# Language-model tower in one kernel: identifiers in two transfers of 128 equal rows, the shift made in the one-hot

## Chip, cores and metric

One core of one Trainium2 chip. The metric is the device time of one execution in microseconds (us); lower is better.

## What is computed

16 sequences of 128 identifiers (0 to 63) and 128 positions go through a token encoder, a diagonal state-space layer and a feed-forward layer with 8 experts, all in float32. The start of the encoder is what matters here:

```python
amps = emb[byte_sequence]
onehot = jnp.transpose(jax.nn.one_hot(byte_sequence, 64), (0, 2, 1))
h = gelu(conv1d(onehot, w1, b1, 3))         # 64 -> 128, 7 taps
h = gelu(conv1d(h, w2, b2, 2))              # 128 -> 64, 5 taps
ctx = sigmoid(conv1d(h, w3, b3, 1))[:, 0, :]
amps = amps * ctx[:, :, None]
lp = locality_shapes[byte_sequence]
center = byte_pos[None, :] + lp[..., 0] * 0.05
xd = continuous_positions[:, None, :] - center[..., None]
...                                         # 4 scales:
z = xd / width[..., None]
basis = exp(-0.5 * z * z) * cos(phase + TWO_PI * z)
...
field = einsum('bsp,bsd->bpd', basis_total, amps)
```

Then `h = field`, `h = h + attn(layernorm(h))`, `h = h + ffn(layernorm(h))`.

## The kernel before, in words

Each engine has its own list of instructions, written out by hand, and runs it strictly in order; semaphores join the lists. The 16 sequences are worked in G = 4 groups of GB = 4 (512 columns), so stage names carry a group: `z(g)`, `product(g)`, `field(g)`.

**Loads.** SyncE issues all loads in a row (L261 to L270): the identifiers twice, w1, positions of group 0 ("pos0"), positions of the others ("pos"), w2, the state constants, wd, bd. ScalarE's queue loads the small constants (L414). The identifiers go to partitions 0 to 63 and again to 64 to 127, each time all 2048 of them, repeated into 64 rows of 8 KB; the lower half of the tile `ids` holds them one element later than the upper half.

**One-hot.** VectorE compares identifiers with the partition's value. `onehot_b` (bf16, 64 partitions, L641) feeds the look-ups: TensorE multiplies it by three bf16 parts of the table, first for the 4 locality shapes (L935 to L937, 48 matmuls), then for the embeddings (`embeddings(q)`, 24 matmuls each). `onehot` (128 partitions, padded, L645 to L649) feeds `conv1`: its upper half is the same one-hot shifted by one position, so that one matmul serves two taps. Its pads are cleared by GpSimd (L299, L300).

**TensorE** fills gaps with `keep_warm(n, bank)`: n matmuls of 512 columns whose result nobody reads (L921). Its list begins: keep_warm(14), look-ups of shapes, keep_warm(3), embeddings(0), keep_warm(3), conv1 of groups 0 and 1, conv1 of groups 2 and 3 (8 matmuls a group, in two parts of w1), conv2(0) (L965), embeddings(1), tap(0), keep_warm(10), context(0), keep_warm(8), conv2(1), keep_warm(4), field(0), keep_warm(6), upright(0), field(1), tap(1), and so on. `upright(g)` transposes the field back (L1004) after ScalarE's `field_out(g)` (L500) copied it; ScalarE's `upright_out(g)` (L504) then writes `h_a`.

**ScalarE** copies the shapes (L442), takes the tanh of one of them (L444), rounds w1 to its first part (L446), negates the centre (L448), then forms the distances of groups 1 to 3 (`distances(g)`, L455, four activations each, all waiting for "pos"). Between these stand conv1_out (L460, gelu), square (L466). Then conv2_out(0) (L482), the exp table, gaussian (L470), cosine (L476, sine table), square(2), cosine(2), field_out(0), load_gelu, upright_out(0), conv2_out(1), load_exp, field_out(1), taps_out(1), gaussian(2), upright_out(1), context_out(1) (L495). `load_gelu`, `load_exp` and `load_sin` run a one-column activation (L425) whose function makes the engine load its table (1.28 us) at that place.

**VectorE**, after the one-hot, forms w1's second part (L651), centre (L655), widths, phase and their reciprocals, the distances of group 0 (L669), and then z(0), z(1), turns(0), turns(1), z(2), turns(2), gates(0), product(0), product(1), z(3), moments(0, 0), turns(3), normalise(0, 0), gates(1), product(2) and on. `z` is L675; `turns` is four operations of phase and wrap (L685) and one mask (L690); `gates(q)` (L715, L722) needs context_out(q); `product` is L732; `moments(0, 0)` (L744, L747) needs `h_a` of group 0; GpSimd then computes the reciprocal standard deviation (L379 to L386) and `normalise(0, 0)` (L754) uses it.

Of the kernel before, what the change touches and what calls it, by code (L numbers as in the profile page):

```python
# [15 lines left out]
ALU = mybir.AluOpType  # L16
ACT = mybir.ActivationFunctionType
F32 = mybir.dt.float32
# [4 lines left out]
P = 128  # L23
# [48 lines left out]
def tower(nc, x, positions, small, w1, w2, state, wd, bd, out):  # L72
    ctx = ExitStack()
    with ctx:
# [27 lines left out]
        ids = sb("ids", [P, NB * P + 2], I32)  # L102
# [29 lines left out]
        center = sb("center", [P, NB])  # L132
# [82 lines left out]
        s_onehot = sem("s_onehot")  # L215
        s_w1_part = sem("s_w1_part")
        s_center, s_warm = sem("s_center"), sem("s_warm")
# [40 lines left out]
        @block.sync  # L258
        def _(sp):
            row = x.rearrange("b t -> (b t)")  # L260
            for half in range(2):  # L261
                sp.dma_start(ids[half * V:half * V + V, 1 - half:1 - half + NB * P],
                             repeat(row, 0, V)).then_inc(ld[f"x{half}"], 16)
            sp.dma_start(w1_sb[:, :, :], w1).then_inc(ld["w1"], 16)
            sp.dma_start(posb[:, 0:GB, :], repeat(positions[0:GB], 0, P)).then_inc(ld["pos0"], 16)
            sp.dma_start(posb[:, GB:, :], repeat(positions[GB:], 0, P)).then_inc(ld["pos"], 16)
            sp.dma_start(w2_sb[:, :, :], w2).then_inc(ld["w2"], 16)
            sp.dma_start(st_sb[:, :], state).then_inc(ld["state"], 16)
            sp.dma_start(wd_sb[:, :, :], wd).then_inc(ld["wd"], 16)
            sp.dma_start(bd_sb[:, :], bd[0].rearrange("(p c) -> p c", p=P)).then_inc(ld["bd"], 16)  # L270
            sp.wait_ge(s_bd_split, 1)
            for half in range(2):
                for k in range(3):
                    row = half * D + k
                    sp.dma_start(bdp[row:row + 1, :].rearrange("o (p c) -> o p c", p=P),
                                 bd_parts[:, k, :]).then_inc(ld["bias"], 16)
            for g in range(G - 1):
                sp.wait_ge(s_result, g + 1)
                sp.dma_start(out[g * GB:(g + 1) * GB].rearrange("b p d -> p b d"),
                             result[:, g]).then_inc(stored, 16)  # L280
            for h in range(2):
                sp.wait_ge(s_last, 2 * h + 2)
                sp.dma_start(out[(G - 1) * GB + h:G * GB:2].rearrange("b p d -> p b d"),
                             result[:, G - 1, h:GB:2]).then_inc(stored, 16)
            sp.wait_ge(stored, 16 * (G + 1))
# [127 lines left out]
        def _(act):  # L413
# [4 lines left out]
            act.activation(half_b3[:, :], col("b3"), ACT.Copy, scale=0.5).then_inc(s_halfb3, 1)  # L418

# [20 lines left out]
            load_gelu()  # L440
            act.wait_ge(s_shapes_mm, 1)
            act.copy(shapes[:, :, :].rearrange("p b c -> p (b c)"), bank[6][:, 0:NB * NL]).then_inc(s_shapes, 1)  # L442
            act.wait_ge(s_shapes, 1)
            act.activation(amp_tanh[:, :], shapes[:, :, 2], ACT.Tanh, scale=0.5).then_inc(s_amp_tanh, 1)  # L444
            act.wait_ge(ld["w1"], 16)
            act.copy(w1p[0][:], w1_sb[:]).then_inc(s_w1_part, 1)  # L446
            act.wait_ge(s_center, 1)
            act.activation(neg_center[:, :], center[:, :], ACT.Copy, scale=-1.0).then_inc(s_negc, 1)  # L448
            act.wait_ge(s_negc, 1)

            def distances(g):

                act.wait_ge(ld["pos"], 16)
                for b in range(g * GB, (g + 1) * GB):
                    ins = act.activation(dist[:, b, :], posb[:, b, :], ACT.Identity, bias=neg_center[:, b:b + 1])  # L455
                ins.then_inc(s_rest[g], 1)
# [83 lines left out]

            distances(1)
            conv1_out(0)
            distances(2)
# [22 lines left out]
            field_out(0)  # L566
            load_gelu()
            upright_out(0)
# [50 lines left out]
        def _(dve):  # L619
            count = [0]  # L620

            def link(ins):
# [15 lines left out]
            dve.wait_ge(ld["x0"], 16)  # L638
            from_first, from_zero = (ids[:, k:k + NB * P].rearrange("p (b t) -> p b t", b=NB) for k in (1, 0))
            value = col("value")  # L640
            dve.tensor_scalar(onehot_b[:, :, :], from_first[0:V], value[0:V], None,  # L641
                              ALU.is_equal).then_inc(s_onehot, 1)
            dve.wait_ge(ld["x1"], 16)
            dve.wait_ge(s_pad, 2)
            dve.tensor_scalar(onehot[:, :, 3:2 + P], from_first[:, :, 0:P - 1], value, None, ALU.is_equal)  # L645
            dve.tensor_scalar(onehot[0:V, :, 2 + P:3 + P], from_first[0:V, :, P - 1:P], value[0:V], None,
                              ALU.is_equal)
            dve.tensor_scalar(onehot[V:, :, 2:3], from_zero[V:, :, 0:1], value[V:], None,
                              ALU.is_equal).then_inc(s_onehot, 1)  # L649
            dve.wait_ge(s_w1_part, 1)  # L650
            dve.tensor_tensor(w1p[1][:], w1_sb[:], w1p[0][:].bitcast(F32), ALU.subtract).then_inc(s_w1_part, 1)  # L651

            dve.wait_ge(s_shapes, 1)
            lp = [shapes[:, :, k] for k in range(NL)]
            dve.tensor_scalar(center[:, :], lp[0], 0.05, col("place"), ALU.mult, ALU.add).then_inc(s_center, 1)  # L655
            link(dve.scalar_tensor_tensor(out=absw[:, :], in0=lp[1], scalar=-1.0, in1=lp[1], op0=ALU.mult, op1=ALU.max))
            for s in range(NS):
                c = SMALL["widths"].start + s
                ins = dve.tensor_scalar(width[:, :, s, :], absw[:, :].rearrange("p (g b) -> p g b", g=G),
                                        sm[:, c:c + 1], 1e-5, ALU.mult, ALU.add)  # L660
            link(ins)
# [3 lines left out]
            dve.scalar_tensor_tensor(out=phase[:, :], in0=lp[3], scalar=0.5, in1=phase_tmp[:, 1, :],  # L665
                                     op0=ALU.mult, op1=ALU.subtract)
            dve.wait_ge(ld["pos0"], 16)
            dve.wait_ge(s_center, 1)
            link(dve.tensor_tensor(dist[:, 0:GB, :], posb[:, 0:GB, :], repeat(center[:, 0:GB], 2, P), ALU.subtract))  # L669

            def z(g):

                if g:
                    dve.wait_ge(s_rest[g], 1)
                dve.tensor_tensor(  # L675
                    wave[:, g, :].rearrange("p (s t) -> p s t", s=NS),
                    repeat(dist[:, g * GB:(g + 1) * GB, :].rearrange("p b t -> p (b t)"), 1, NS),
                    repeat(inv_width[:, g, :, :].rearrange("p s b -> p (s b)"), 2, P),
                    ALU.mult).then_inc(s_z[g], 1)

            def turns(g):
# [7 lines left out]
                link(ins)  # L689
                dve.tensor_scalar(angle[:, g, :], angle[:, g, :], TURN_MASK, None,  # L690
# [163 lines left out]
            turns(0)  # L854
            turns(1)
            z(2)
            turns(2)
# [3 lines left out]
            z(3)  # L861
            moments(0, 0)
            turns(3)
# [53 lines left out]
        def _(pe):  # L917
# [6 lines left out]
            keep_warm(14, 7)  # L924

            pe.wait_ge(s_emb_split, 1)
            pe.wait_ge(s_onehot, 1)
# [7 lines left out]
            for b in range(NB):  # L935
                mm = look_up(bank[6][:, b * NL:(b + 1) * NL], b, slice(D, D + NL))
# [192 lines left out]
            pe.wait_ge(s_onehot, 2)  # L1129
            conv1((0, 1))  # L1130
            conv1((2, 3))
# [143 lines left out]
```

## Time and profile before

| | us |
|---|---|
| runs, median (lowest to highest) | 111.62 (111.35 to 115.62) |
| the profiled execution | 111.52 |
| its span in the profile | 109.6 |
| busy TensorE, VectorE, ScalarE, GpSimd | 100.5, 90.0, 70.8, 51.0 |

All durations below are of the one profiled execution. The span is the time from the first to the last recorded instruction; the rest of the execution's time lies around it. TensorE's busy time holds the keep_warm matmuls.

### The profile page before, as it was taken

How to read it: one execution, taken by the hardware profiler on the slowest of the kernel's cores; microseconds unless marked ns; L12 is line 12 of the kernel's file. 1: busy time of each engine (PE TensorE's matmuls, PEld its weight loads, DVE VectorE, ACT ScalarE, POOL GpSimd, SP SyncE). 2: the span in 40 equal slices, each digit the busy share in tenths (PEclk: the TensorE clock that was granted, in tenths of full speed). 3: DMA queues.
4: the chain of work that ended last, by engine and by line, in shares of the span. 5: the costliest groups of instructions: out<-in, count | busy, mean ns of one | idle time of the engine just before them, and what ended most of it. 6: DMA issues, size and time to landing. Idle time of an engine off the chain costs nothing.

```text
span 109.6 us, 2018 instructions
## 1 busy us (share of the span) xinstructions
PE 100.5 (92%) x723; PEld 64.3 (59%) x723; DVE 90.0 (82%) x230; ACT 70.8 (65%) x126; POOL 51.0 (47%) x101
## 2 busy tenths in 40 slices
PE   5979999999999978869899999999999799999970
PEld 2356785364434576347567477876696476776640
DVE  0359999999999949999999599678999956199892
ACT  4604599999999999999869438454758513551000
POOL 7798998899980007205509426256005000000670
PEclk9999999999999999999999999999999999999999
DMA  3999700000000100000000000000000000000044
GB/s 91 269 233 408 283 0 0 3 0 0 6 0 4 5 0 0 0 0 6 0 0 0 0 6 0 0 0 0 0 0 9 0 0 0 0 0 0 0 96 96
DMA packets 4313, 4.15 MB, mean 38 GB/s; under 512 B 3280, under 2 KB 3536, under 8 KB 4176
## 3 DMA queue, kind: packets, MB, share of 16 engines
q1 hardware_dynamic: 4160, 3.92, 12.5%
q10 hardware_dynamic: 144, 0.12, 0.4%
q8 instruction: 5, 0.08, 0.3%
q14 instruction: 4, 0.03, 0.1%
HBM read 3.50 MB, written 0.52 MB: 37 GB/s over the span
## 4 chain that ended last, share of the span: by engine, by line
PE 42%; ACT 38%; DVE 8%; DMA 4%; issue 4%; POOL 2%; ACTq 0%; DVEq 0%
PE pair L1080 14%; ACT wave L476 8%; PE bank L1042 7%; ACT bell L466 7%; ACT bell L470 5%; ACT L425 5%; DMA ids<-x 4%; DVE pair L819 3%; PE hid_pair L1053 3%; PE pair L951 3%; ACT angle L514 3%; PE pair L921 2%; ACT h L460 2%; PE hid_pair L1063 2%; ACT dist L455 2%
## 5 line engine op out<-in xcount | busy, mean ns | idle before, releaser
L379 POOL TENSOR_SCALAR var_eps<-mean_var 128x4 f32<-128x4 f32 x8 | 3.7, 458 | 33.0 <-DVE mean_var L747 33.0
L819 DVE COPY_PREDICATED pair<-later,pair 128x256 f32<-128x256 int32 (+3 forms) x30 | 12.3, 409 | 5.3 <-PE pair L1080 4.6
L921 PE MATMUL pair<-warm 128*128 128x512 bf16 x53 | 13.3, 380 | 0.0
L732 DVE SCALAR_TENSOR_TENSOR bell<-bell,scale_w,wave 128x512 f32<-128x512 f32 x16 | 10.8, 743 | 0.0
L1080 PE MATMUL pair<-wd_high,H_high 128*128 128x512 f32 x32 | 10.8, 418 | 0.0
L921 PE MATMUL hid_pair<-warm 128*128 128x512 bf16 x30 | 9.0, 455 | 1.3 <-POOL warm L298 1.3
L1080 PE MATMUL pair<-wd_low,H_high 128*128 128x512 f32 x32 | 10.0, 394 | 0.0
L395 POOL TENSOR_TENSOR angle<-picked,prob 128x256 f32<-128x256 f32 x3 | 1.8, 613 | 17.2 <-DVE prob L843 17.2
L521 ACT ACTIVATE bell<-hid_pair,sm 128x512 f32<-128x512 f32 x8 | 5.0, 680 | 7.2 <-PE hid_pair L1053 7.2
L675 DVE TENSOR_TENSOR wave<-dist,inv_width 128x2048 f32<-128x2048 f32 x4 | 9.3, 2356 | 0.0
L965 PE MATMUL pair<-h,w_sb 128*64 128x512 f32 x40 | 9.1, 597 | 0.0
L1080 PE MATMUL pair<-wd_high,H_low 128*128 128x512 f32 x32 | 9.0, 402 | 0.0
L476 ACT ACTIVATE wave<-angle,neg_pi 128x1024 f32<-128x1024 int32 x8 | 8.6, 1138 | 0.1
L385 POOL TENSOR_TENSOR rstd<-var_eps,minus_half 128x4 f32<-128x4 f32 x6 | 8.2, 1366 | 0.0
L685 DVE TENSOR_SCALAR angle<-wave,phase 128x512 int32<-128x512 f32 x16 | 8.0, 561 | 0.0
L921 PEld LDWEIGHTS pair<-warm 128*128 128x128 bf16 x53 | 4.9, 102 | 5.2 <-issue 1.3
L951 PE MATMUL pair<-onehot,w1p 128*128 128x512 f32 x32 | 7.9, 404 | 0.0
L996 PE MATMUL pair<-bell,amps 128*64 128x128 f32 x128 | 7.9, 276 | 0.0
L425 ACT ACT_TABLE_LOAD x6 | 7.7, 1283 | 0.1
L996 PEld LDWEIGHTS pair<-bell,amps 128*64 128x64 f32 x128 | 6.9, 137 | 1.3 <-issue 1.3
L470 ACT ACTIVATE bell<-bell 128x2048 f32<-128x2048 f32 x4 | 7.6, 1920 | 0.0
L466 ACT ACTIVATE bell<-wave 128x2048 f32<-128x2048 f32 x4 | 7.6, 1910 | 0.0
(166 smaller groups left out, 226.1 us busy)
## 6 DMA issues: line engine op xcount, KB each, us to landing
ids<-x SPq DMA_DIRECT2D x2, 512.0 KB, 5.7
posb<-positions SPq DMA_DIRECT2D x1, 768.0 KB, 8.1
wd_sb<-wd SPq DMA_DIRECT2D x1, 512.0 KB, 9.1
out<-angle SPq DMA_DIRECT2D x3, 128.0 KB, 2.0
st_sb<-state SPq DMA_DIRECT2D x1, 328.0 KB, 8.3
w_sb<-w SPq DMA_DIRECT2D x1, 256.0 KB, 6.6
posb<-positions SPq DMA_DIRECT2D x1, 256.0 KB, 6.6
w_sb<-w SPq DMA_DIRECT2D x1, 160.0 KB, 8.0
```

Source lines behind the costliest of these rows:

```text
L425: act.activation(unused[:, k:k + 1], neg_pi[:, :], function)
L466: act.activation(bell[:, g, :], wave[:, g, :], ACT.Square).then_inc(s_square[g], 1)
L470: act.activation(bell[:, g, :], bell[:, g, :], ACT.Exp, scale=-0.5).then_inc(s_bell[g], 1)
L476: act.activation(wave[:, g, part], angle[:, g, part], ACT.Sin, bias=neg_pi[:, 0:1], scale=2.0 * PI_BELOW / TURN).then_inc(s_cos[g], 1)
L675: dve.tensor_tensor(wave[:, g, :].rearrange("p (s t) -> p s t", s=NS), repeat(dist[:, g * GB:(g + 1) * GB, :].rearrange("p b t -> p (b t)" ...
L732: ins = dve.scalar_tensor_tensor(out=bell[:, g, part], in0=bell[:, g, part], scalar=scale_w[:, s:s + 1], in1=wave[:, g, part], op0=ALU.mul ...
L819: return dve.copy_predicated(held[:, :, 0:n, 0, 0:D], repeat(later[:, g, 2 * h + rows.start:2 * h + rows.stop, first:first + n], 3, D), he ...
L921: pe.matmul(bank[free], warm[:, 0:P], warm[:, :], start=True, stop=True)
L951: mm = pe.matmul(bank[g], w1p[part][:, j, :], onehot[:, g * GB:(g + 1) * GB, 2 * j:2 * j + P], start=(part == 0 and j == 0), stop=(part == ...
L965: mm = pe.matmul(bank[2 * q][r * D:(r + 1) * D, :], w2_sb[:, k, :], h1[:, g * GB:(g + 1) * GB, k:k + P], start=(k == 0), stop=(k == K2 - 1))
L996: mm = pe.matmul(bank[g][r * D:(r + 1) * D, c * P:(c + 1) * P], amps[:, g * GB + b, :], bell[:, g, at:at + P], start=(s == 0), stop=(s == ...
L1080: mm = pe.matmul(pair[h][:, jj, :], hidden_part[:, g % 2, k, cols], weights[:, k, :], start=False, stop=last and k == KH - 1)
```

## The change

- Identifiers: two transfers again, but each carries half of the text (8 sequences, 1024 identifiers) to all 128 partitions, in rows of 4 KB; `ids` is no longer shifted.
- One-hot by halves of the text: VectorE makes `onehot_b` (64 partitions) and then the upper, shifted rows of `onehot` (the shift is now in where it writes). ScalarE copies `onehot_b` to the lower rows. conv1 waits for both, by halves.
- TensorE: 11 warm-up matmuls at the start in place of 14; the shape look-ups in two halves with 4 warm-up matmuls between; embeddings(0) stays before conv 1.
- VectorE makes the negated centre itself (with a negated place that ScalarE prepares early), and w1's second part after the widths. ScalarE makes all four groups' distances, group 0 waiting only for "pos0"; the order is distances(0), amp tanh, distances(1), distances(2), conv1_out(0).
- `turns` is split into `phases` and `wrap`, which follow each other but for group 3: z(3), phases(3), moments(0, 0), wrap(3).
- ScalarE: upright_out(0) stands before load_gelu in place of behind it.

```diff
@@ sync
-            for half in range(2):
-                sp.dma_start(ids[half * V:half * V + V, 1 - half:1 - half + NB * P],
-                             repeat(row, 0, V)).then_inc(ld[f"x{half}"], 16)
+            for part in range(2):
+                n = slice(part * NB * P // 2, (part + 1) * NB * P // 2)
+                sp.dma_start(ids[:, n], repeat(row[n], 0, P)).then_inc(ld[f"x{part}"], 16)
@@ scalar
+            act.activation(neg_place[:, :], col("place"), ACT.Copy, scale=-1.0).then_inc(s_place, 1)
...
+            act.wait_ge(s_pad, 2)
+            for part in range(2):
+                n = slice(part * NB // 2, (part + 1) * NB // 2)
+                act.wait_ge(s_onehot, part + 1)
+                act.copy(onehot[0:V, n, 3:3 + P], onehot_b[:, n, :]).then_inc(s_lower, 1)
             act.wait_ge(s_shapes_mm, 1)
             act.copy(shapes[:, :, :].rearrange("p b c -> p (b c)"), bank[6][:, 0:NB * NL]).then_inc(s_shapes, 1)
             act.wait_ge(s_shapes, 1)
-            act.activation(amp_tanh[:, :], shapes[:, :, 2], ACT.Tanh, scale=0.5).then_inc(s_amp_tanh, 1)
             act.wait_ge(ld["w1"], 16)
             act.copy(w1p[0][:], w1_sb[:]).then_inc(s_w1_part, 1)
-            act.wait_ge(s_center, 1)
-            act.activation(neg_center[:, :], center[:, :], ACT.Copy, scale=-1.0).then_inc(s_negc, 1)
             act.wait_ge(s_negc, 1)
...
-                act.wait_ge(ld["pos"], 16)
+                act.wait_ge(ld["pos" if g else "pos0"], 16)
...
+            distances(0)
+            act.activation(amp_tanh[:, :], shapes[:, :, 2], ACT.Tanh, scale=0.5).then_inc(s_amp_tanh, 1)
             distances(1)
+            distances(2)
             conv1_out(0)
-            distances(2)
             conv1_out(1)
...
             field_out(0)
+            upright_out(0)
             load_gelu()
-            upright_out(0)
             conv2_out(1)
@@ vector
-            dve.wait_ge(ld["x0"], 16)
-            from_first, from_zero = (ids[:, k:k + NB * P].rearrange("p (b t) -> p b t", b=NB) for k in (1, 0))
+            ids_rows = ids[:, :].rearrange("p (b t) -> p b t", b=NB)
             value = col("value")
-            dve.tensor_scalar(onehot_b[:, :, :], from_first[0:V], value[0:V], None,
-                              ALU.is_equal).then_inc(s_onehot, 1)
-            dve.wait_ge(ld["x1"], 16)
-            dve.wait_ge(s_pad, 2)
-            dve.tensor_scalar(onehot[:, :, 3:2 + P], from_first[:, :, 0:P - 1], value, None, ALU.is_equal)
-            dve.tensor_scalar(onehot[0:V, :, 2 + P:3 + P], from_first[0:V, :, P - 1:P], value[0:V], None,
-                              ALU.is_equal)
-            dve.tensor_scalar(onehot[V:, :, 2:3], from_zero[V:, :, 0:1], value[V:], None,
-                              ALU.is_equal).then_inc(s_onehot, 1)
-            dve.wait_ge(s_w1_part, 1)
-            dve.tensor_tensor(w1p[1][:], w1_sb[:], w1p[0][:].bitcast(F32), ALU.subtract).then_inc(s_w1_part, 1)
+            for part in range(2):
+                n = slice(part * NB // 2, (part + 1) * NB // 2)
+                dve.wait_ge(ld[f"x{part}"], 16)
+                dve.tensor_scalar(onehot_b[:, n, :], ids_rows[0:V, n], value[0:V], None,
+                                  ALU.is_equal).then_inc(s_onehot, 1)
+                if part == 0:
+                    dve.wait_ge(s_pad, 2)
+                dve.tensor_scalar(onehot[V:, n, 2:2 + P], ids_rows[V:, n], value[V:], None,
+                                  ALU.is_equal).then_inc(s_upper, 1)
...
+            dve.wait_ge(s_place, 1)
-            dve.tensor_scalar(center[:, :], lp[0], 0.05, col("place"), ALU.mult, ALU.add).then_inc(s_center, 1)
+            dve.tensor_scalar(neg_center[:, :], lp[0], -0.05, neg_place[:, 0:1], ALU.mult,
+                              ALU.add).then_inc(s_negc, 1)
...
+            dve.wait_ge(s_w1_part, 1)
+            dve.tensor_tensor(w1p[1][:], w1_sb[:], w1p[0][:].bitcast(F32), ALU.subtract).then_inc(s_w1_part, 1)
...
-            link(dve.tensor_tensor(dist[:, 0:GB, :], posb[:, 0:GB, :], repeat(center[:, 0:GB], 2, P), ALU.subtract))
...
             z(3)
+            phases(3)
             moments(0, 0)
-            turns(3)
+            wrap(3)
             normalise(0, 0)
@@ tensor
-            keep_warm(14, 7)
+            keep_warm(11, 7)
             pe.wait_ge(s_emb_split, 1)
-            pe.wait_ge(s_onehot, 1)
...
-            for b in range(NB):
-                mm = look_up(bank[6][:, b * NL:(b + 1) * NL], b, slice(D, D + NL))
+            for part in range(2):
+                pe.wait_ge(s_onehot, part + 1)
+                for b in range(part * NB // 2, (part + 1) * NB // 2):
+                    mm = look_up(bank[6][:, b * NL:(b + 1) * NL], b, slice(D, D + NL))
+                if part == 0:
+                    keep_warm(4, 7)
             mm.then_inc(s_shapes_mm, 1)
...
-            pe.wait_ge(s_onehot, 2)
+            pe.wait_ge(s_lower, 1)
+            pe.wait_ge(s_upper, 1)
             conv1((0, 1))
+            pe.wait_ge(s_lower, 2)
+            pe.wait_ge(s_upper, 2)
             conv1((2, 3))
```

## Rows read from the trace of the kernel before

**Rows 1.** Chain of waits that ended last: start us, us, what; its first transfer.
```profile
0.72 4.86 DMA ids<-x
```

**Rows 2.** DMA issues: out<-in engine op xcount, KB each, us from issue to landing.
```profile
posb<-positions SPq DMA_DIRECT2D x1, 768.0 KB, 8.1
...
posb<-positions SPq DMA_DIRECT2D x1, 256.0 KB, 6.6
```

**Rows 3.** Timeline of SyncE's queue and TensorE: start us, us, engine, line, op.
```profile
1.30 5.07 PE L921 MATMUL hid_pair<-warm 128*128 128x512 bf16 x14 [1.30 <-POOL warm L298]
...
2.62 0.43 SPq L265 DMA_DIRECT2D posb<-positions  x1
3.09 0.44 SPq L266 DMA_DIRECT2D posb<-positions  x1
...
5.11 0.76 PEld L921 LDWEIGHTS hid_pair<-warm 128*128 128x128 bf16 x4 [0.28 <-issue]
...
8.34 0.82 PE L921 MATMUL hid_pair<-warm 128*128 128x512 bf16 x3
...
10.36 7.90 PE L951 MATMUL pair<-onehot,w1p 128*128 128x512 f32 x32
...
18.19 4.52 PE L965 MATMUL pair<-h,w_sb 128*64 128x512 f32 x20
```

**Rows 4.** Timeline of VectorE up to z(0) and z(1).
```profile
5.61 1.31 DVE L641 TENSOR_SCALAR onehot_b<-ids,sm 64x2048 bf16<-64x2048 int32 x1 [1.54 <-DMA ids<-x]
7.95 1.30 DVE L645 TENSOR_SCALAR onehot<-ids,sm 128x2032 fp32r<-128x2032 int32 x1 [1.03 <-DMA ids<-x]
...
10.29 0.23 DVE L655 TENSOR_SCALAR center<-shapes,sm 128x16 f32<-128x16 f32 x1
...
13.07 4.52 DVE L675 TENSOR_TENSOR wave<-dist,inv_width 128x2048 f32<-128x2048 f32 x2
```

**Rows 5.** Timeline of ScalarE: conv1_out(0), distances(2), conv2_out(0), a cast of 128x1024.
```profile
13.59 0.69 ACT L460 ACTIVATE h<-pair,sm 128x512 f32<-128x512 f32 x1 [1.05 <-PE pair L951]
14.18 1.27 ACT L455 ACTIVATE dist<-posb,neg_center 128x128 f32<-128x128 f32 x4
...
22.91 0.69 ACT L482 ACTIVATE h<-pair,sm 128x512 f32<-128x512 f32 x1
...
57.95 1.03 ACT L589 CAST wd_high<-wd_sb 128x1024 fp32r<-128x1024 f32 x1
```

**Rows 6.** Busy time by stretch: stretch, PE busy (x) PEld DVE ACT POOL, PEclk, DMA, GB/s.
```profile
22.90:38.60 15.70, 15.15 (x116) 7.53 (x111) 15.56 (x19) 15.55 (x17) 9.33 (x13) 1.00 0.04 3
...
46.30:53.60 7.30, 5.90 (x49) 3.49 (x48) 7.20 (x20) 6.84 (x9) 2.97 (x4) 1.00 0.01 2
```

**Rows 7.** Timeline of ScalarE and VectorE, 38 to 46 us.
```profile
38.52 0.35 ACT L500 COPY angle<-pair 128x256 f32<-128x256 f32 x1
...
40.29 0.35 ACT L504 COPY h_a<-pair 128x256 f32<-128x256 f32 x1
40.54 0.69 ACT L482 ACTIVATE h<-pair,sm 128x512 f32<-128x512 f32 x1
40.68 0.60 DVE L744 BATCH_NORM_STATS2 stats<-h_a 128x6 f32<-128x64 f32 x4 [1.45 <-ACT h_a L504]
...
41.61 1.64 DVE L685 TENSOR_SCALAR angle<-wave,phase 128x512 int32<-128x512 f32 x4
...
44.59 0.98 DVE L754 TENSOR_SCALAR angle<-h_a,mean_var,rstd 128x64 f32<-128x64 f32 x4
...
45.05 0.29 ACT L495 ACTIVATE ctx_tanh<-hid_pair,half_b 128x8 f32<-128x8 f32 x1
...
45.49 0.16 DVE L715 SCALAR_TENSOR_TENSOR gain<-ctx_tanh,amp_tmp 128x8 f32<-128x8 f32 x1
```

**Rows 8.** Timeline of ScalarE: field_out(3) and upright_out(3) without a table load between them.
```profile
60.58 0.35 ACT L500 COPY angle<-pair 128x256 f32<-128x256 f32 x1
...
61.47 0.38 ACT L504 COPY h_a<-pair 128x256 f32<-128x256 f32 x1
```

More of the change, by code:

```diff
@@ L101, in tower @@
         posb = sb("posb", [P, NB, P])
-        ids = sb("ids", [P, NB * P + 2], I32)
+        ids = sb("ids", [P, NB * P], I32)
         def col(name):
@@ L131, in tower @@
         amps = sb("amps", [P, NB, D])
-        center = sb("center", [P, NB])
+        neg_place = sb("neg_place", [P, 1])
         absw = sb("absw", [P, NB])
@@ L214, in tower @@
         s_emb_split = sem("s_emb_split")
-        s_onehot = sem("s_onehot")
+        s_onehot, s_lower, s_upper = sem("s_onehot"), sem("s_lower"), sem("s_upper")
         s_w1_part = sem("s_w1_part")
-        s_center, s_warm = sem("s_center"), sem("s_warm")
+        s_place, s_warm = sem("s_place"), sem("s_warm")
         s_copied = [sem("s_copied0"), sem("s_copied1")]
@@ L664, in _ @@
             link(dve.tensor_scalar(phase_tmp[:, 1, :], phase_tmp[:, 0, :], -ROUND, -0.75, ALU.add, ALU.add))
[L665 to L668, printed above, removed]
-            link(dve.tensor_tensor(dist[:, 0:GB, :], posb[:, 0:GB, :], repeat(center[:, 0:GB], 2, P), ALU.subtract))
+            link(dve.scalar_tensor_tensor(out=phase[:, :], in0=lp[3], scalar=0.5, in1=phase_tmp[:, 1, :],
+                                          op0=ALU.mult, op1=ALU.subtract))
             def z(g):
-                if g:
-                    dve.wait_ge(s_rest[g], 1)
+                dve.wait_ge(s_rest[g], 1)
                 dve.tensor_tensor(
@@ L679, in z, with phases @@
                     ALU.mult).then_inc(s_z[g], 1)
-            def turns(g):
+            def phases(g):
                 dve.wait_ge(s_z[g], 1)
@@ L689, in turns, with wrap @@
                 link(ins)
+            def wrap(g):
                 dve.tensor_scalar(angle[:, g, :], angle[:, g, :], TURN_MASK, None,
@@ L853, in _ @@
             z(1)
-            turns(0)
-            turns(1)
-            z(2)
-            turns(2)
+            phases(0)
+            wrap(0)
+            phases(1)
+            wrap(1)
+            z(2)
+            phases(2)
+            wrap(2)
             gates(0)
```

## Prediction

> **What bounds the kernel now.** I read the chain of waits first. It begins with the identifiers' transfer, issued at 0.72 and landed at 5.58 [rows 1]. The busy times by stretch show what leads then: ScalarE is busy for 15.55 of the 15.70 us from 22.9 to 38.6, VectorE for 7.20 of the 7.30 from 46.3 to 53.6 [rows 6], and behind it the chain stays mostly on TensorE. So the question is in two parts: how much earlier can ScalarE get into its long run (conv2_out(0), at 22.91 [rows 5]), and does what it gains there live until VectorE's product(2) at 46.3, behind which everything later hangs?
>
> For the second part I read the timeline around 38 to 46 us. There two engines are level. ScalarE ends context_out(1) at 45.34; VectorE takes it up in gates(1) at 45.49, when its own normalise(0, 0) (44.59, 0.98 long) is just over [rows 7]. A change must move both to move the end.
>
> **The transfers.** The two transfers of now carry 512 KB each (64 partitions, rows of 8 KB). The first lands at 5.58; the second at 7.93, since VectorE's wait for it ends at 7.95 [rows 4]: 2.35 us, 223 GB/s. The two loads of positions, repeated rows as well but on 128 partitions, land at 2.62 + 6.6 = 9.2 and 3.09 + 8.1 = 11.2: 768 KB in 2.0 us, 393 GB/s [rows 2, 3]. At that pace 512 KB take 1.33 us. The new first transfer should land about 1 us of moving earlier; as part of its 4.86 us is start-up, shared with the small constants, I take 0.7 of it: 4.9. The second comes 1.33 later, 6.2. Bounds: no faster than now (5.58 and 7.93), or all of the first's gain (4.6 and 5.9).
> The Trainium skill's SBUF page (SBUF — State Buffer, Door 1: the DMA port swizzle) says that 64 partitions reach half of the ports, for about 218 GB/s, and 128 all, for 436; by it 512 KB would take 1.2 us. Its DMA page (DMA: Bandwidth & Descriptors, Specifications) speaks against so much: about 358 GB/s from HBM, which would make it 1.46 us. The trace's 393 lies between, and is measured.
>
> **One-hot on VectorE.** Now 64x2048 takes 1.31 us and 128x2032 1.30 [rows 4]. Four operations of 64x1024 replace them: half of 1.31 is 0.66, all of it would be 1.31; I take 0.76, a little over half for the fixed part. The first half's bf16 one-hot is ready at 4.93 + 0.76 = 5.69, its upper rows at 6.4, the second bf16 half at 7.1 (the second transfer has long landed), its upper rows at 7.8. Now the last piece ends at about 9.65.
>
> **TensorE up to conv 1.** Warm-up matmuls come first, 11 in place of 14. The 14 took 5.07 us from 1.30; weight loads come every 0.43 us up to 5.11, where the last four begin together [rows 3]. So ten run at 0.427 (1.2 GHz for 512 columns) and four in 0.8 (2.4 GHz); I go by these steps. Eleven end at 1.30 + 4.27 + 0.2 = 5.78: however early the identifiers come, nothing starts sooner. By the one-hot, the first 24 look-ups start at 5.69 + 0.14 = 5.83. The 48 take 1.28 us (7.06 to the next warm-up at 8.34), so 24 take 0.64: 6.47. Then four warm-ups at 0.25: 7.47. Then 24 more: 8.11. From there to conv 1 all is as now, 3 warm-ups, 24 look-ups, 3 warm-ups, 8.34 to 10.36 = 2.02 [rows 3]. Conv 1 starts at 10.13, which is 0.23 us earlier; at best, by the 5.78, 0.28.
> Conv 1's other inputs come in time. ScalarE's lower-row copies, 64x1024, have 128x1024 as nearest row, 1.03 us [rows 5]: 5.7 to 6.75 and 7.1 to 8.15. The look-ups' copy follows at 8.2 and takes 0.2, then the first part of w1, half the length of that row, some 0.6: done by 9.1. VectorE's second part of w1, moved behind the widths, ends by 10.4 and is asked for 2 us into conv 1. If the copies took twice as long, w1 would be ready at about 10.2 to 11.2 and conv 1 up to 1 us late; that end I keep for the range.
>
> **VectorE and ScalarE up to conv2_out(0).** VectorE goes from centre to z(0) in 13.07 - 10.29 = 2.78 [rows 4]. It starts at about 8.5, loses the distances (128x512) and gains the w1 part (128x512, two inputs as well): z(0) at 11.3, 1.8 us earlier. distances(0), new on ScalarE, needs four activations, 1.27 us as distances(2) does [rows 5], from 9.15 to 10.4, and delays nothing. ScalarE waited 1.05 us for conv 1 at 13.59 [rows 5]; this gap takes distances(2) and the rest. With conv 1 at 10.13 it does conv1_out(0) at 13.3, square(0) at 14.9, conv1_out(2, 3) by 19.15, and would reach conv2_out(0) at 22.05, some 0.9 us earlier. But the convolution itself isn't there: conv 2 starts straight behind conv 1, at 18.19, and ends at 22.71 [rows 3], so now at 22.48. conv2_out(0) starts at 22.51 and not at 22.91: **gain 0.40 us**, and 0.5 us of ScalarE's lead goes into a wait on TensorE.
>
> **ScalarE 22.9 to 45.3.** All stays in order and without idle [rows 6] up to field_out(0), which comes 0.40 earlier (38.12). Here the change pulls upright_out(0) in front of the load of the gelu table. Now ScalarE hides TensorE's transposes behind that 1.28 us load: field_out(0) at 38.52, upright_out(0) at 40.29, conv2_out(1) at 40.54, a step of 2.02 [rows 7]. Where upright_out follows field_out with no load between, the second starts 0.89 after the first (60.58 and 61.47) [rows 8]. From a copy over a table load to the next operation it is 1.77 (38.52 to 40.29). The new step is 0.89 + 1.77 = 2.66: **loss 0.64 us**. The cover is gone and nothing takes its place. Sum at conv2_out(1): -0.40 + 0.64 = +0.24. Its tap and context follow in the same order, so context_out(1) ends at 45.58.
>
> **VectorE 39 to 46.** It waited 1.45 us, from 39.23, for h_a(0) [rows 7]. Now phases(3) (1.64) stands in that wait, and h_a(0) is ready at about 39.3. Even with z(3) not earlier, moments(0, 0) begins at 40.87; GpSimd's rstd then takes the 2.9 us of now or, with VectorE quiet, less. normalise(0, 0) ends between 44.7 and 45.7, so the context decides: gates(1) at 45.6 in place of 45.49, **+0.1 us**. VectorE's lead of up to 1.8 us turns into waits there. The new wait of ScalarE for the transposes has conv2_out(1), tap(1) and context(1) queued behind it; this is its price, already counted.
> From product(2) on the order and the work are the same, VectorE and then TensorE bound, and all shifts by that 0.1. phases and wrap are the same instructions under two names; field, experts and the tail are untouched. Field_out(1) to cosine(3) on ScalarE are 0.24 late, with cosine(3) done by about 53.1 while product(3) reads its first half at 53.4: free.
>
> **Sum.** The profiled execution took 111.52, with 109.6 of span and 1.9 around it; it stands 0.1 under the median of 111.62. 111.52 + 0.1 gives **111.6 us**, no change that can be told. Its own range, from the 4.6 landing and the 0.64 in full or two thirds of it, is 111.2 to 112.0.
>
> **Rivals.**
> A. *The identifiers don't come faster, and the split costs*: what sets their pace would be the repeated read or the count of rows, not the partitions. For it: twice the rows to handle; against: the 393 GB/s of positions. Landings 5.58 and 7.93; second bf16 half at 7.95 + 0.76 = 8.7; look-ups end at 9.5; conv 1 at 11.5, +1.1. conv2_out(0) is then at 23.6 to 23.8 (+0.9 at most, since conv 2 had 0.2 of lead), plus 0.64 for the table load, makes context_out(1) +1.5: **113.0**, slower. It decides as soon as the second one-hot half is later than 7.3, when TensorE begins to wait. VectorE in a full-length 1.31 us for 64x1024 comes to the same place.
> B. *The wait for the upright copy isn't paid*: were the transposes ready when ScalarE asks, the 0.40 would go through. ScalarE at 44.94, VectorE ready at 44.7 to 44.9, gates(1) at 44.95, 0.54 earlier: **111.0**. For it: VectorE waited 1.45 us for this very result, so it was wanted sooner. Against: TensorE can't begin before field_out(0), and the 0.89 step [rows 8] is bare latency.
> C. *The whole lead of VectorE counts* (1.8 us, 109.7), if the chain's pieces on ScalarE were only parallel. Against: ScalarE has no idle from 22.9 to 38.9, and gates(1) must have the context.
>
> **Chances.** Forecast 0.62, A 0.15, B 0.18, C 0.05. The range goes from 110.8 (below B) to 113.0 (A's time, and most of the late copies). A difference of 2% is about what a measurement of this kernel can tell from none; faster by more (under 109.4) has 0.04, between C and nothing; slower by more (over 113.85) 0.04, if A and late copies add up; within 0.92.
>
> **What would show it.** Right: the first one-hot operation near 4.9 and the second half's near 6.4; conv 1's first matmul at 10.1; z(0) at 11.3; ScalarE idle for about 0.5 us in front of conv2_out(0), at 22.5, and again in front of upright_out(0) on its way to the table load; conv2_out(1) near 40.8; VectorE idle ahead of gates(1) near 45.6. Wrong: conv 1 after 10.5 (A); conv2_out(1) before 40.3 (B); product(2) before 45.5.

## The result: slower by 3.6%, and the profile after

| | before | changed |
|---|---|---|
| median of the runs, us | 111.53 | 116.47 |
| lowest to highest | 111.35 to 115.62 | 114.73 to 118.08 |
| the profiled execution | 111.52 | 116.83 |
| its span | 109.6 | 114.7 |

Four executions of each kernel stand in the table (three of the kernel before in the table ahead of the prediction, hence 111.62 there). The ratio is 1.0355, 95% interval 1.0205 to 1.0505; forecast was 111.6. The ratio leaves out the two most disturbed of the changed kernel's four runs, the profiled one among them; its spread and TensorE's mean granted clock, 0.956 to 0.985 in the four, are part of what is explained below.

First the DMA issues of the changed kernel (KB each, us from issue to landing):

```profile
ids<-x SPq DMA_DIRECT2D x2, 512.0 KB, 5.1
...
sm<-small ACTq DMA_DIRECT2D x1, 116.0 KB, 4.8
```

The identifiers did what was forecast: 4.6 and 5.5 us from issues at 0.72 and 1.15, so 5.3 and 6.6, 1.3 us apart (forecast 4.9 and 6.2, 1.33 apart). But the small constants, 116 KB on ScalarE's queue, landed at 5.54. In the kernel before, the same load landed at 2.83. The DMA queues' packets, MB and busy share from 1.5 to 2.5 us show how, first before, then changed (q1 is SyncE's queue, q10 ScalarE's; the share is of the time of 16 DMA engines):

```profile
q1 hardware_dynamic: 16, 0.13, 59.7%
q10 hardware_dynamic: 144, 0.12, 46.6%
```

```profile
q1 hardware_dynamic: 42, 0.17, 50.0%
q10 hardware_dynamic: 11, 0.01, 8.2%
```

Before, all 144 packets of the constants pass in this microsecond; changed, 11 of them, and the last one only after 5.0. Two chains start from them: VectorE's split of the table, without which there are no look-ups, and GpSimd's some 25 operations on one column each (L325 to L351) that compute the coefficients of the state-space layer, here called the poles. ScalarE's `decay` activation, which stands ahead of conv2_out(0), waits for the poles. Timeline of the changed kernel, VectorE and TensorE:

```profile
5.56 0.19 DVE L636 CAST embp<-sm 64x68 bf16<-64x68 f32 x1 [5.56 <-DMA sm<-small]
...
6.72 0.74 DVE L648 TENSOR_SCALAR onehot_b<-ids,sm 64x1024 bf16<-64x1024 int32 x1
...
7.61 0.74 PE L939 MATMUL hid_pair<-embp,onehot_b 64*128 64x4 bf16 x24 [1.43 <-DVE onehot_b L648]
...
9.95 1.46 PE L930 MATMUL hid_pair<-warm 128*128 128x512 bf16 x3
...
11.34 1.46 PE L939 MATMUL bank<-embp,onehot_b 64*128 64x64 bf16 x24
...
13.63 9.17 PE L963 MATMUL pair<-onehot,w1p 128*128 128x512 f32 x32
22.73 4.52 PE L977 MATMUL pair<-h,w_sb 128*64 128x512 f32 x20
```

TensorE, done with its 11 warm-ups, idled 1.43 us ahead of the first look-ups (1.8 us later than forecast). From 9.95 on it ran at half pace: three warm-ups in 1.46 us against 0.82 [rows 3]. The busy times by stretch of the changed kernel (PEclk is the first number behind POOL's) name it:

```profile
8.00:10.00 2.00, 2.00 (x43) 1.30 (x41) 1.75 (x3) 1.54 (x2) 1.89 (x3) 0.91 1.01 369
10.00:12.00 2.00, 2.00 (x17) 0.89 (x17) 1.67 (x9) 1.97 (x7) 1.82 (x4) 0.50 0.88 344
12.00:14.00 2.00, 2.00 (x19) 1.27 (x17) 1.90 (x5) 2.00 (x9) 1.71 (x4) 0.50 0.07 21
14.00:16.00 2.00, 2.00 (x6) 1.63 (x5) 2.00 (x2) 0.55 (x2) 1.92 (x2) 0.50 0.00 0
16.00:18.00 2.00, 2.00 (x9) 1.56 (x9) 2.00 (x3) 0.00 (x0) 2.00 (x2) 0.88 0.00 0
```

The granted clock is at its lower level, 1.2 GHz, for some 7 us. Conv 1 starts at 13.63 in place of 10.36 and takes 9.17 in place of 7.90. The next fence has one operation of GpSimd's chain in the kernel before; the one behind it has that operation and the next of the changed kernel, and its ScalarE:

```profile
9.93 0.88 POOL L339 TENSOR_TENSOR spar<-spar,minus_half 128x1 f32<-128x1 f32 x1
```

```profile
12.96 2.69 POOL L339 TENSOR_TENSOR spar<-spar,minus_half 128x1 f32<-128x1 f32 x1
15.73 1.74 POOL L340 TENSOR_TENSOR spar<-spar 128x1 f32<-128x1 f32 x1
...
26.37 0.73 ACT L557 ACTIVATE decay<-decay,spar 128x512 f32<-128x512 f32 x1 [0.68 <-POOLq L352]
...
27.48 0.67 ACT L485 ACTIVATE h<-pair,sm 128x512 f32<-128x512 f32 x1
...
43.06 0.35 ACT L503 COPY angle<-pair 128x256 f32<-128x256 f32 x1
43.94 0.37 ACT L507 COPY h_a<-pair 128x256 f32<-128x256 f32 x1 [0.53 <-PE pair L1016]
...
45.73 0.67 ACT L485 ACTIVATE h<-pair,sm 128x512 f32<-128x512 f32 x1
```

VectorE of the changed kernel, gates(1):

```profile
50.53 0.17 DVE L720 SCALAR_TENSOR_TENSOR gain<-ctx_tanh,amp_tmp 128x8 f32<-128x8 f32 x1 [0.74 <-ACT ctx_tanh L498]
```

conv2_out(0) is 4.57 us late against 22.91 [rows 5]. From there the forecast's sum holds to a tenth: 4.57 and 0.64 for the transposes, less the 0.15 that VectorE had to spare, is 5.06. gates(1) is 5.04 late (50.53 against 45.49 [rows 7]), the span 5.1.

### The profile page after: what moved, and what is told of

The parts are those of the page before. It is cut to its first block, busy times and chain, and to the rows that moved or that the text cites. A ratio compares the mean times of both kernels' runs of the same rounds, so it can differ in the third digit from the quotient of the medians.

```text
span 114.7 us, 2029 instructions
## 1 busy us (share of the span) xinstructions
PE 104.0 (91%) x724; PEld 66.2 (58%) x724; DVE 87.3 (76%) x229; ACT 74.1 (65%) x132; POOL 50.8 (44%) x101
## 4 chain that ended last, share of the span: by engine, by line
PE 35%; ACT 23%; POOL 19%; DVE 11%; issue 5%; DMA 4%; ACTq 0%; POOLq 0%; DVEq 0%
PE pair L1092 14%; PE bank L1054 6%; ACT wave L479 6%; DMA sm<-small 4%; ACT L426 3%; DVE pair L824 3%; POOL spar L347 3%; ACT bell L473 3%; PE hid_pair L1065 3%; ACT angle L517 2%; DVE bell L737 2%; POOL spar L339 2%; PE pair L930 2%; PE hid_pair L1075 2%; PE bank L1037 2%
## 5 line engine op out<-in xcount | busy, mean ns | idle before, releaser
L930 PE MATMUL hid_pair<-warm 128*128 128x512 bf16 x31 | 11.1, 516 | 1.3 <-POOL warm L298 1.3
L737 DVE SCALAR_TENSOR_TENSOR bell<-bell,scale_w,wave 128x512 f32<-128x512 f32 x16 | 10.9, 745 | 1.4 <-ACT wave L479 1.4
L963 PE MATMUL pair<-onehot,w1p 128*128 128x512 f32 x32 | 9.2, 450 | 0.0
L963 PEld LDWEIGHTS pair<-onehot,w1p 128*128 128x128 f32 x32 | 7.0, 220 | 2.0 <-issue 0.3
```

The lines of the kernel that those rows point to most:

```text
L737: ins = dve.scalar_tensor_tensor(out=bell[:, g, part], in0=bell[:, g, part], scalar=scale_w[:, s:s + 1], in1=wave[:, g, part], op0=ALU.mul ...
L930: pe.matmul(bank[free], warm[:, 0:P], warm[:, :], start=True, stop=True)
L963: mm = pe.matmul(bank[g], w1p[part][:, j, :], onehot[:, g * GB:(g + 1) * GB, 2 * j:2 * j + P], start=(part == 0 and j == 0), stop=(part == ...
```

## Experiments

Each ratio is to the kernel before, run beside the experiment: its median was 111.45 beside e1 to e4, 111.58 beside e5, e6, e7 and e10, and 112.51 beside e8 and e9, each group on a chip of its own. Times of single stages are of the one profiled execution.

**Constants first, on the same queue.** e1, the changed kernel with:

```diff
@@ sync
+            sp.dma_start(sm[:, :], small).then_inc(ld["small"], 16)
@@ scalar
-            act.dma_start(sm[:, :], small).then_inc(ld["small"], 16)
```

> The changed kernel, with the small constants loaded as the first transfer of SyncE's queue and no longer from ScalarE's. Theory 1 (the constants, 116 KB, are mixed with the identifiers' rows and land at 5.54 instead of 2.83; all that starts from them is late): they land by about 3.2, the first look-ups start at 5.8 to 6.2, TensorE is never at half clock, conv 1 starts at 10.1 to 10.5, and the time is 111.3 to 112.2, as was forecast for the change. Theory 2 (the split one-hot with its ScalarE copies and 11 warm-ups costs by itself): conv 1 still at half clock or after 12, the time 114 or more.

```profile
2.89 0.19 DVE L636 CAST embp<-sm 64x68 bf16<-64x68 f32 x1 [2.89 <-DMA sm<-small]
...
6.29 0.74 PE L939 MATMUL hid_pair<-embp,onehot_b 64*128 64x4 bf16 x24 [0.48 <-DVE onehot_b L648]
...
10.64 7.88 PE L963 MATMUL pair<-onehot,w1p 128*128 128x512 f32 x32
```

Profiled 112.81, span 110.2, ratio 1.0079 (1.0013 to 1.0146). The constants land early, conv 1 runs at full clock. Conv 1's start is 0.14 outside the expected interval, since the identifiers, now behind the constants, land at 5.4; the time is 0.6 above its interval. Theory 1 holds for the bulk: 4.0 of the 5.3 us between the profiles are gone. But of six runs two took 115.4 and 115.6 with a mean clock of 0.97, which was not expected: early constants alone don't make the kernel safe.

**More warm-ups.** e2, the changed kernel with `keep_warm(18, 7)` for `keep_warm(11, 7)` at the start.

> The changed kernel with 18 warm-up matmuls in place of 11 at the start, so that TensorE's idle 1.4 us before the first look-ups is gone while the constants are as late as before. If the fall of the clock comes from that idle time: no stretch at half clock, conv 1 starts near 11.8 in place of 13.6 and takes 7.9 us in place of 9.2. If it comes from the low activity of the warm-ups and look-ups as such, the clock falls all the same. For the time: if TensorE's late conv 1 was the only thing that held conv2_out(0), the time falls by about 3 us, to 112 to 113; if GpSimd's chain of poles (ready at 26.3, also started by the late constants) holds ScalarE's decay just as late, conv2_out(0) stays near 27.3 and the time within 0.5 us of the changed kernel's.

```profile
5.57 0.19 DVE L636 CAST embp<-sm 64x68 bf16<-64x68 f32 x1 [5.57 <-DMA sm<-small]
...
11.97 7.87 PE L963 MATMUL pair<-onehot,w1p 128*128 128x512 f32 x32
...
26.36 0.72 ACT L557 ACTIVATE decay<-decay,spar 128x512 f32<-128x512 f32 x1 [3.65 <-POOLq L352]
27.46 0.67 ACT L485 ACTIVATE h<-pair,sm 128x512 f32<-128x512 f32 x1
```

TensorE's idle time before the look-ups shrank to 0.38 us and conv 1 ran at full clock, 1.7 us earlier and 1.3 shorter. In the profiled execution it brought nothing: ScalarE waited 3.65 us for GpSimd's poles, and conv2_out(0) stayed at 27.46. Profiled 117.18. From 22 to 30 us, where TensorE now idled 3.1 us, the mean granted clock was 0.94, and from 46 to 53 us 0.76. Three of the four runs took 117.2 to 118.7. The fourth, not profiled, took 113.86 with a clock of 1.00; its span of 111.8 leaves no room for conv2_out(0) as late as that, and why isn't known.

**Both holds away.** e10, the same 18 warm-ups, and ScalarE's three activations on GpSimd's values (`decay` and two `C_part`, L552 to L555 of the kernel before) moved from ahead of conv2_out(0) to behind cosine(1).

> The changed kernel with 18 warm-up matmuls, and with ScalarE's decay and C_part activations, which wait for GpSimd's poles, moved from ahead of conv2_out(0) to behind cosine(1). Constants are late as in the changed kernel. If the clock and the poles were the two holds on conv2_out(0), it starts near 24.4 (conv 2's end) in place of 27.48, and the time falls by about 2.5 to 3.3 us against the changed kernel, to 113.3 to 114.3. If only one of the two or a third one held it, it stays at or above 26.

```profile
24.16 0.69 ACT L485 ACTIVATE h<-pair,sm 128x512 f32<-128x512 f32 x1 [1.62 <-PE pair L977]
...
40.86 0.35 ACT L503 COPY angle<-pair 128x256 f32<-128x256 f32 x1
```

Profiled 114.65, 2.2 less than changed, runs 114.54 to 115.64, ratio to before 1.0303 (1.0269 to 1.0337): the start of conv2_out(0) is 0.24 earlier than expected, the time 0.35 above its interval, the gain 0.3 short. The rows have the missing part: conv2_out(0) came 3.3 us earlier, but the three moved activations now stand behind it, and field_out(0) starts 16.7 us after it in place of 15.6. So there were two holds, the half clock and the poles. That the poles alone are late enough is e2. That the half clock alone is, no run of the changed kernel's load order shows, but two others do: in e5 and e6 below the constants and the poles were early, TensorE went at half pace, and conv2_out(0) waited for conv 2 until 27.90. In the changed kernel itself conv 2 ends at 27.25.

**Warm-ups alone.** e3, the kernel before with `keep_warm(11, 7)` for `keep_warm(14, 7)`.

> The kernel before with 11 warm-up matmuls in place of 14: TensorE then idles about 1.0 to 1.3 us (5.8 or 6.2 to 7.06) with the constants early and everything else as it was. If an idle stretch at this point takes the clock down, conv 1 runs partly at half clock, starts up to 1.5 us later and ends up to 4 us later, time 113 to 115.5. If the clock stays: 111.5, no change.

```profile
8.00:10.00 2.00, 2.00 (x25) 0.92 (x22) 1.95 (x4) 0.95 (x3) 1.86 (x3) 0.60 1.08 430
10.00:12.00 2.00, 2.00 (x24) 1.36 (x21) 1.90 (x10) 1.02 (x4) 1.73 (x6) 0.55 1.02 389
```

Profiled 112.82, median 113.05, ratio 1.0145 (1.0115 to 1.0176); the interval began at 113. TensorE idled 1.36 us to 7.00, the granted clock was at its lower level from about 8.4 to 11.8, conv 1 started at 11.84, as expected. Three dummy matmuls less cost 1.3 us between the profiles and 1.45% by the ratio, in a kernel that is otherwise the same.

**Rows of 64 partitions.** e4, the changed kernel with the transfers of before:

```diff
-                sp.dma_start(ids[:, n], repeat(row[n], 0, P)).then_inc(ld[f"x{part}"], 16)
+                sp.dma_start(ids[part * V:part * V + V, :],
+                             repeat(row, 0, V)).then_inc(ld[f"x{part}"], 16)
```

(VectorE's waits follow: both halves of `onehot_b` wait for the first transfer, the upper rows for the second.)

> The changed kernel with the two transfers of the kernel before (whole text, 64 partitions, 8 KB rows); one-hot, copies and order stay as changed, the upper rows wait for the second transfer. Theory 1: the constants land again near 2.8, TensorE idles little and the clock stays, conv 1 near 11.3 to 12 for lack of the second half's one-hot, the time 112.5 to 113.5. If the constants are late for another reason (their own queue, the earlier issue of the later loads), they land at 5 or later here too and the time is 115 or more.

```profile
2.87 0.19 DVE L636 CAST embp<-sm 64x68 bf16<-64x68 f32 x1 [2.87 <-DMA sm<-small]
...
9.51 0.75 PE L940 MATMUL hid_pair<-embp,onehot_b 64*128 64x4 bf16 x24 [1.38 <-DVE onehot_b L648]
...
13.76 7.90 PE L964 MATMUL pair<-onehot,w1p 128*128 128x512 f32 x32
```

The constants land early again, from the same queue at the same instant, so it is the new form of the identifiers' transfers beside them that held them up. Which part of the form, 128 partitions for 64 or rows of 4 KB for 8, isn't separated: e4 takes back both. (The loads behind go back to their old issue times too, w1 to 2.00 from 1.63, but the 42 packets of SyncE's queue that pass first in the changed kernel carry 4 KB each, as the identifiers' rows do.) The expectations for TensorE and the time missed (profiled 115.43, ratio 1.0381, 1.0314 to 1.0448): the upper rows had to wait for the second transfer at 7.9, VectorE's second half stood behind them, TensorE idled 1.38 us until 9.5, and the granted clock fell behind that (0.58 and 0.56 from 10 to 14 us); conv 1 started at 13.76 and not by 12. I had left the clock out of that sum.

**Who is issued first.** e6, the changed kernel; SyncE waits for GpSimd's first memset ahead of the identifiers:

```diff
+            sp.wait_ge(s_warm, 1)
```

> The changed kernel; SyncE waits for GpSimd's first memset (done at 1.25 us) before it issues the identifiers, so that ScalarE's constants are issued half a microsecond ahead of them. If only who is first decides, the constants land near 2.9, identifiers near 5.6, conv 1 starts near 10.9, the clock stays, time 112 to 113. If the rows of two queues are mixed whoever comes first, since the constants' own rows are short: constants at 4 or later, time 114 or more.

```profile
2.88 0.19 DVE L637 CAST embp<-sm 64x68 bf16<-64x68 f32 x1 [2.88 <-DMA sm<-small]
...
6.00 0.78 DVE L649 TENSOR_SCALAR onehot_b<-ids,sm 64x1024 bf16<-64x1024 int32 x1 [1.88 <-DMA ids<-x]
...
6.92 0.77 PE L940 MATMUL hid_pair<-embp,onehot_b 64*128 64x4 bf16 x24 [0.75 <-DVE onehot_b L649]
7.62 1.89 PE L931 MATMUL hid_pair<-warm 128*128 128x512 bf16 x4
```

On the constants the answer is clear: half a microsecond of lead and they land at 2.88, with the 128-row transfers unchanged. On the time it isn't: 111.98 in one run, 117.15 to 117.9 in three, where 112 to 113 was expected. In the profiled one (117.49) the identifiers came at 5.98, TensorE idled 0.75 us behind its 11 warm-ups, the four warm-ups that followed took 1.89 us, 0.47 each, half pace, and conv 1 started at 13.86 in place of the expected 10.9.

**ScalarE's new wait.** e7, the kernel before with upright_out(0) ahead of load_gelu; e5, the kernel of e1 with it behind again.

> The kernel before with one edit: ScalarE's upright_out(0) in front of the gelu table load. By the forecast's term: conv2_out(1) 0.64 us later at 41.2, context_out(1) ends at 46.0, VectorE's gates(1) moves from 45.49 to about 46.0, the time rises by 0.5, to 112.0. Rival (the earlier h_a(0) was worth more): the time falls, to 111.0.

> The changed kernel with the constants first on SyncE's queue, as in the first experiment, and ScalarE's upright_out(0) back behind the gelu table load. If the wait for the transposes costs what was forecast (0.64 us on ScalarE, less 0.1 that VectorE's normalise(0, 0) then holds): conv2_out(1) starts 2.02 after field_out(0) in place of 2.66, gates(1) near 45.4 in place of 46.1, the time 0.5 to 0.7 under the first experiment's, 111.3 to 112.2. If VectorE, which gets h_a(0) later again, takes over at once: no gain over the first experiment.

e7, profiled 112.07, ratio 1.0043 (1.0026 to 1.0060):

```profile
39.43 0.37 ACT L504 COPY h_a<-pair 128x256 f32<-128x256 f32 x1 [0.53 <-PE pair L1004]
...
41.22 0.67 ACT L482 ACTIVATE h<-pair,sm 128x512 f32<-128x512 f32 x1
...
46.02 0.17 DVE L715 SCALAR_TENSOR_TENSOR gain<-ctx_tanh,amp_tmp 128x8 f32<-128x8 f32 x1 [1.29 <-ACT ctx_tanh L495]
```

The term stands as forecast: conv2_out(1) 0.68 later, gates(1) at 46.02, the time 0.5 longer. The earlier h_a(0) is worth nothing, it turns into 1.29 us of VectorE's waiting. e5's time can't be read for it: 111.77 to 116.25, ratio 1.0115 (1.0068 to 1.0162), profiled 116.25 where 111.3 to 112.2 was expected. Its identifiers landed at 6.28, TensorE idled 1.01 us after 11 warm-ups and went at half pace. The step itself can be read, and it came as expected: field_out(0) at 43.51, conv2_out(1) at 45.53, 2.02 us in place of e1's 2.67. The last two lines are its ScalarE, with the wait for conv 2:

```profile
7.90 1.89 PE L930 MATMUL hid_pair<-warm 128*128 128x512 bf16 x4
...
14.13 9.27 PE L963 MATMUL pair<-onehot,w1p 128*128 128x512 f32 x32
...
27.90 0.69 ACT L485 ACTIVATE h<-pair,sm 128x512 f32<-128x512 f32 x1 [0.54 <-PE pair L977]
...
45.53 0.69 ACT L485 ACTIVATE h<-pair,sm 128x512 f32<-128x512 f32 x1
```

**The change mended.** e8 is e5 with `keep_warm(15, 7)`; e9 is e8 with embeddings(0) moved:

```diff
-            keep_warm(3, 7)
-            embeddings(0)
-            keep_warm(3, 7)
+            keep_warm(4, 7)
             pe.wait_ge(s_lower, 1)
...
             tap(0)
-            keep_warm(10, 6)
+            embeddings(0)
+            keep_warm(7, 6)
```

(VectorE's gates then wait for both embeddings.)

> Constants first on SyncE's queue, upright_out(0) behind the table load, and 15 warm-up matmuls in place of 11, which end near 6.4 to 6.6, when the first half of the look-ups can begin (6.3 to 7.2 in the runs so far). If the spread of the runs (111.8 to 116.3) came from TensorE's idle time before the look-ups and the fall of its pace behind it: no run at half pace, all within 0.5 us, median 111.3 to 112.0. If not: runs of 115 and more again.

> The same, and embeddings(0) with its warm-ups no longer ahead of conv 1 but behind tap(0), where it takes the place of 3 of 10 warm-ups; 4 warm-ups stand ahead of conv 1. Conv 1 can then start when ScalarE has the first part of w1, near 9.7 in place of 10.6; conv2_out(0) gains the 0.54 us that ScalarE waited for conv 2 and no more, so the time is 0.4 to 0.6 under that of the kernel with 15 warm-ups alone: 110.8 to 111.5, level with the kernel before or just under it.

e8: twelve runs, 111.73 to 113.34, median 112.05, ratio 0.9987 (0.9950 to 1.0024), profiled 111.73. No run over 114: the mean clock is 0.994 or more in all twelve. In the profile the four more warm-ups cost nothing, since the 15th ends 0.29 us before the look-ups start. The median is 0.05 above its interval, and the expected spread of half a microsecond was too narrow (0.8, and one run of 113.34). Of the kernels with early constants and 11 warm-ups, e1 and e5, four runs in twelve took over 114; with 15 warm-ups none of eighteen did (e8, e9), though on another chip, and the kernel before, with 14, had three such runs in 45. gates(1) is at 45.55, 0.55 before e1's 46.10: the term of the transposes once more.

e9: 110.44 to 111.86, median 111.32, ratio **0.9886** (0.9841 to 0.9931), against a median of 112.51 of the kernel before on that chip. Most of that 1.1% is this median: on the two other chips it was 111.45 and 111.58, and the profiles are 111.39 for e9 and 111.52 for the kernel before, the spans 109.4 and 109.6. e9's timeline:

```profile
6.05 0.75 DVE L648 TENSOR_SCALAR onehot_b<-ids,sm 64x1024 bf16<-64x1024 int32 x1 [1.97 <-DMA ids<-x]
...
10.50 7.80 PE L963 MATMUL pair<-onehot,w1p 128*128 128x512 f32 x32
...
45.26 0.17 DVE L720 SCALAR_TENSOR_TENSOR gain<-ctx_tanh,amp_tmp 128x8 f32<-128x8 f32 x1
```

Although its identifiers landed 0.6 us later than e8's, conv 1 began 0.2 earlier; the 9.7 that was expected had the identifiers as early as e8's. ScalarE still waited 0.53 us for conv 2, so that part of the expectation failed. And the cover reached its end on the other side: here the 15 warm-ups took 5.82 us, to 7.12, and the look-ups started 0.25 us behind their one-hot in place of e1's 0.14. It is the one version whose ratio lies clear of 1 on the faster side; how much of that is the version's own isn't settled.

## Why the prediction was wrong

- **The constants' landing** is the step that failed. The forecast wrote that the first transfer shares its start-up with the small constants and priced that for the identifiers alone (0.7 of 1 us). For the constants it had no term at all: it took them as landed, 2.83 as before, without a word. They landed at 5.54. The profile of before showed them first through; that this hung on the form of their neighbour, no step asked. What e4 and e6 show: with 64 rows of 8 KB beside them, or with 128 rows of 4 KB issued half a microsecond later, they land at 2.9. Why the form decides stays open. The Trainium skill's page DMA: Bandwidth & Descriptors, in Queues, rings and completion order, says that each of the 16 engines goes round the queues that it has work for, a packet from each, and gives no price for it (its packet may hold several of the profile's). The changed kernel's counts from 2.5 to 4.5 us agree (39 and 76 packets of the constants beside 33 and 77 of SyncE's queue); the 144 beside 16 of the kernel before, in the microsecond from 1.5, aren't equal turns.
- **TensorE up to conv 1.** 5.83 + 2 x 0.64 + 1.0 + 2.02 = 10.13 was a sum of busy times at full clock. With the constants early, e1 gave 10.64, the rest being the identifiers' 5.4 in place of 4.9. What the sum had no term for is the clock. The 11 warm-ups were read only as the earliest time for the look-ups, 5.78; what TensorE does when the look-ups come later had no price, though the forecast let the warm-ups end just as the first half's one-hot came (5.78 and 5.83). Any lateness then turns into idle time, and behind the changed kernel's 1.43 us came 7 us at the lower level: 3.0 us of conv 1's late end (13.63 + 9.17 = 22.8, against 19.8 in e2 with constants as late). The forecast's list of one-hot pieces (6.4, 7.1, 7.8) also gives each 0.71 us where it took 0.76; that is 0.1 to 0.2 us on the second half, which the look-ups asked for only at 7.47, so it cost nothing.
- **GpSimd's chain** of poles has no term in the forecast. Ready at 18.2 before, it was ready at 26.3: 2.7 us of late start, and 5.4 of lengthened operations (L339 took 2.69 us beside VectorE's z in place of 0.88), with most of the chain now behind the start of z(0). That this is what lengthened them is read from the rows and wasn't tested. e2 and e10 show that it alone holds conv2_out(0) at 27.5.
- **The rivals.** A had the right direction (slower, 113.0) by a wrong cause: the identifiers moved as fast as forecast, 1.3 us a transfer (512 KB in 1.3 us is 403 GB/s; positions had run at 393). That A came nearer is luck. B is refuted by e7, C by e1, where z(0) began 1.4 us earlier than before and gates(1) 0.6 later. None of the three had anything in it of what lies beside the identifiers, so the range ended 1.7 us under the fastest run.
- **Right:** the one-hot pieces (0.74 to 0.76 us; 0.76 taken), the lower copies (1.05; 1.03), the step over the transposes (2.67; 2.66), the end at the context and not at VectorE (gates(1) waits 0.74 us for it), ScalarE's wait of about 0.5 us for conv 2 (0.54 in e1 and e8). With the constants ahead and the clock kept (e1) gates(1) is 0.61 late in place of 0.1, and the difference is conv 1's start, 10.64 for 10.13. The span is 0.6 longer; the profiled time is 1.3 longer, since 0.7 more than before lies outside the span, which no row explains.

## What to carry to other kernels

A load is priced together with what is issued beside it: if a transfer's rows change, look which small load on another queue passed ahead of it until now, and what starts from that load; put it first on the same queue or give it a lead. Warm-up matmuls are a cover with an end: count them to the latest, not the earliest, landing of what they wait for. Four more cost nothing in one profile and 0.1 us in the other, and no run over 114 us came with them. When a late input starts two chains, mending one of them can show nothing, as e2 did.

## What the runs showed of the hardware

**TensorE's pace behind idle time.** The length of the idle time doesn't tell by itself whether the pace falls. The table has the warm-ups at the start, the idle time ahead of the first look-ups, and the pace behind it, by the steps of the next 128x512 warm-ups (0.25 us full, 0.47 half) and by the granted clock:

| run | warm-ups, us | idle, us | pace behind |
|---|---|---|---|
| e9 | 15, 5.82 | 0 | full |
| e4 | 11, 4.87 | 0.21 | full |
| e8 | 15, 4.76 | 0.29 | full |
| e2 | 18, 5.94 | 0.38 | full |
| e10 | 18, 5.72 | 0.40 | full |
| e1 | 11, 4.51 | 0.48 | full |
| before | 14, 5.07 | 0.69 | full |
| e6 | 11, 4.87 | 0.75 | half at once |
| e5 | 11, 4.88 | 1.01 | half at once |
| e7 | 14, 4.77 | 1.01 | full |
| e3 | 11, 4.34 | 1.36 | full for 1.4 us, then half |
| changed | 11, 4.87 | 1.43 | full for 2.0 us, then half |

Eleven warm-ups that take 4.87 us ran at 1.2 GHz to the end; where a number took less (14 in 4.77, 11 in 4.34), the last of them ran at 2.4 GHz. When in the row of warm-ups the pace rose differs between executions of the same instructions, and so does the identifiers' landing: with the same loads in the same order it came at 5.4 (e1), 6.3 (e5), 5.4 (e8) and 6.0 us (e9). A cover has to hold for both.

In e5 and e6 the recorded granted clock was 1.00 throughout, while the four warm-ups took 1.89 us instead of 1.04. The row of e5's stretch shows it, so steps between matmuls are to be read beside the clock:

```profile
8.00:10.00 2.00, 2.00 (x14) 0.61 (x14) 1.36 (x2) 1.24 (x2) 1.79 (x4) 1.00 1.02 409
```

**The constants.** Their 116 KB took 2.1 to 2.4 us from issue to landing in nine profiles (before, e1, e3 to e9) and 4.6 to 4.8 in three (changed, e2, e10), all three with 128-row transfers issued in the same instant on the other queue; there is nothing in between.

**GpSimd's chain.** The same 25 or so operations on one column took, from the first (L325) to the last, 10.1 to 10.4 us where they ended within 0.2 us of the start of VectorE's z(0) (e4, e5, e6, e7), 15.0 in the kernel before, and 20.4 in the changed one, where z(0) began 7.0 us behind the chain's start. The kernels of before and of e7 are the same up to there; in e7 the chain ended at 13.8, with z(0) beginning at 13.6. So a start that is 2.7 us late made this chain of tiny operations 8.1 us late.
